# Scores and projections in split 16-bit halves, with weights scaled by bounds and a constant output scale, in a differential-attention block

## The reference, cut to what matters

```python
h = layernorm(x)
qkv = h @ Wqkv.T + b           # 16 query heads and 8 key heads of 128, 4 value heads of 256
p1 = softmax(causal(q1 @ k1.T / sqrt(128)))
p2 = softmax(causal(q2 @ k2.T / sqrt(128)))
o = (p1 - lam * p2) @ v        # 8 pairs of query heads, 256 wide
o = o * rsqrt(mean(o * o) + eps) * subln_w * (1 - LAMBDA_INIT)
x = x + layernorm(o @ out_w.T + out_b)
x = x + layernorm(ffn(layernorm(x)))
```

## Time and profile before

| | |
|---|---|
| median of 3 runs | 1268.17 us |
| the profiled execution, its own time | 1270.65 us |
| its span in the profile | 1268.8 us |
| mean granted clock of TensorE | 0.991 |
| PE busy | 1202.4 us (95%) |
| DVE busy | 1021.7 us (81%) |
| ACT busy | 997.8 us (79%) |
| POOL busy | 780.3 us (62%) |
| chain that ended last | PE 56%, DVE 17%, POOL 8%, issue 6%, ACT 5%, DMA 5% |

### The profile page before, as it was taken

How to read it: one execution, slowest core, us unless ns; L and a number is a source line. 1 busy time by engine, 2 the same in 40 slices (tenths; PEclk the granted TensorE clock), 3 DMA queues, 4 the chain that set the end, 5 groups by cost and what they waited for, 6 DMA issues and landing times.

```text
span 1268.8 us, 26516 instructions
## 1 busy us (share of the span) xinstructions
PE 1202.4 (95%) x8102; PEld 1011.7 (80%) x8102; DVE 1021.7 (81%) x2620; ACT 997.8 (79%) x2607; POOL 780.3 (62%) x1045
## 2 busy tenths in 40 slices
PE   7899999999999999999899999999998898999998
PEld 6788788888878888788788888788876787777887
DVE  6888988888779898988688888778788998846545
ACT  4799889988689989988688888887887898856341
POOL 3576666655657675646476575455567986776532
PEclk9999999999999999999999999999998998999999
DMA  3245554563266555534655554534563555540001
GB/s 130 65 78 103 88 97 93 93 103 71 45 122 105 88 95 90 107 58 64 121 86 91 88 96 85 101 55 82 117 105 86 90 99 94 97 88 1 29 18 38
DMA packets 368154, 106.62 MB, mean 84 GB/s; under 512 B 359312, under 2 KB 365712, under 8 KB 367504
## 3 DMA queue, kind: packets, MB, share of 16 engines
q1 hardware_dynamic: 366672, 103.37, 44.8%
q10 hardware_dynamic: 1344, 1.57, 0.4%
HBM read 14.71 MB, written 2.10 MB: 13 GB/s over the span
## 4 chain that ended last, share of the span: by engine, by line
PE 56%; DVE 17%; POOL 8%; issue 6%; ACT 5%; DMA 5%; SPq 1%; ACTq 0%; POOLq 0%; DVEq 0%
PE score_bank L1039 7%; PE score_bank L1173 6%; PE score_bank L1045 6%; PE score_bank L1042 6%; DVE p L1453 5%; DVE mx L1442 4%; POOL e_all L1736 3%; PE turn_bank L1066 3%; PE turn_bank L1067 3%; PE turn_bank L1068 3%; DMA oT<-o 3%; ACT e_all L1212 2%; DMA p16T<-p 2%; DVE score_bank L1437 2%; PE turn_bank L1119 2%
## 5 line engine op out<-in xcount | busy, mean ns | idle before, releaser
L1212 ACT ACTIVATE e_all<-score_bank,negmx 128x512 f32<-128x512 f32 (+2 forms) x640 | 393.6, 623 | 52.4 <-DVE negmx L1446 36.8
L1736 POOL TENSOR_TENSOR e_all<-e_all 128x512 f32<-128x512 f32 (+3 forms) x320 | 367.8, 1162 | 40.4 <-ACT e_all L1227 30.5
L1039 PE MATMUL score_bank<-k_hi,q_hi 128*128 128x512 f32 (+2 forms) x640 | 255.9, 400 | 27.8 <-ACT e_all L1212 15.5
L1453 DVE SCALAR_TENSOR_TENSOR p<-e_all,gain,p 128x512 f16<-128x512 f32 (+3 forms) x320 | 261.2, 831 | 11.3 <-ACT p L1234 10.5
L1442 DVE TENSOR_REDUCE mx<-score_bank 128x1 f32<-128x512 f32 (+1 forms) x384 | 242.1, 638 | 26.2 <-PE score_bank L1045 25.4
L1042 PE MATMUL score_bank<-k_lo,q_hi 128*128 128x512 f32 (+2 forms) x640 | 232.4, 363 | 0.4 <-DVE k_lo L1503 0.4
L1045 PE MATMUL score_bank<-k_hi,q_lo 128*128 128x512 f32 (+2 forms) x640 | 232.5, 363 | 0.0
L1234 ACT ACTIVATE p<-e_all,gain 128x512 f16<-128x512 f32 (+3 forms) x320 | 204.2, 666 | 20.4 <-POOL e_all L1736 19.7
L1781 POOL TENSOR_SCALAR ratio<-s,inv,neg_lam 128x1 f32<-128x1 f32 x128 | 55.9, 437 | 256.1 <-DVE inv L1724 255.8
L1039 PEld LDWEIGHTS score_bank<-k_hi,q_hi 128*128 128x128 f32 x640 | 121.3, 189 | 66.4 <-issue 27.5
L1066 PE MATMUL turn_bank<-v,p16T 128*128 128x256 f16 x567 | 157.1, 277 | 3.4 <-DVE o L1483 1.3
(11 more groups left out here) (391 smaller groups left out, 2789.0 us busy)
## 6 DMA issues: line engine op xcount, KB each, us to landing
p16T<-p SPq DMA_TRANSPOSE x320, 3.1
w_raw<-in_w_qkv_dram SPq DMA_DIRECT2D x3, 1024.0 KB, 5.4
w_raw<-in_w_o_dram SPq DMA_DIRECT2D x4, 512.0 KB, 3.3
oT<-o SPq DMA_TRANSPOSE x128, 2.5
bv<-in_hidden_dram SPq DMA_DIRECT2D x8, 256.0 KB, 3.0
w_raw<-in_w_ug_dram SPq DMA_DIRECT2D x4, 512.0 KB, 4.0
out_dram<-e SPq DMA_DIRECT2D x16, 128.0 KB, 1.7
e<-in_w_d_dram SPq DMA_DIRECT2D x1, 1024.0 KB, 6.2
```

The lines of the kernel that those rows point to most:

```text
L1039: pe.matmul(bank[:, 0:w], qh, kh, start=True, stop=False)
L1212: act.activation(e, S[k % NS][:, 0:w], ACT.Exp, bias=negmx[:, d % 2, m, s:s + 1], scale=-1.0 if alone else 1.0, accum_out=ssum[:, d % 4, s ...
L1453: dve.scalar_tensor_tensor(out=halves_of(q, w)[1], in0=e1_of(q, w), scalar=gain[:, d % 4, s:s + 1], in1=halves_of(q, w)[0], op0=ALU.mult, ...
L1736: pool.tensor_tensor(a, a, b, ALU.add).then_inc(p_pool, 1)
```

## The change

Input x (times a constant 8), the weights of q, k and v, and q and k themselves are stored as pairs of f16 halves in place of fp32r ones; the matmuls of scores and projections read these. Their number stays (CV has two small matmuls per group in place of one). The FFN's matmuls stay fp32r.

Since f16 has a small range, all three weights are scaled by bounds: per group there is a new step CQ (ACT, sum of squares of WQ), CV on DVE has five sums in place of two, CS on POOL takes the power of three numbers and scales the biases, and CU (DVE, four small instructions) gives `unit`, the factor by which a score must be multiplied. WQ, WK and WV now wait for CS. The exponential takes `unit` as a second pointer operand in 576 of 640 cases, and DVE multiplies the maximum by it (line 1466, 192 instructions that did not exist).

The outputs' halves OH and OL are scaled by the constant 2^-15; OH waits for the last PV alone. VE is gone from DVE; POOL adds the epsilon and multiplies (line 1758) ahead of its power (1761), and the result is applied at the sum into `acc` (1565). The FFN's input has storage of its own, so that its transposes wait for fewer late scores. The planner's costs change (exponential 0.23 to 0.32 us plus the same slope, scores and projections cheaper), and with them the order and the sharing of E2: 186 on ACT and 134 on POOL, where 205 and 115 were.

```diff
-SCORE_US, VALUE_US = 0.00136, 0.00257
+SCORE_US, VALUE_US = 0.00129, 0.00257
...
-                    add("E", "ACT", "E", (d, m, jj), 0.23 + 0.00084 * ww, [("DVE", "S", what)] + room, 1)
+                    add("E", "ACT", "E", (d, m, jj), 0.32 + 0.00084 * ww, [("DVE", "S", what)] + room, 1)
...
-                add("N", "DVE", "VE", o, 0.13, [("ACT", "SQ", o)], 0)
-                add("R", "ACT", "OH", o, 0.37, [("POOL", "OT", o)] + ([("SP", "OX", o - 4)] if o >= 4 else []), 0)
+                add("P", "ACT", "OH", o, 0.28, [pe] + ([("SP", "OX", o - 4)] if o >= 4 else []), 0)
...
-                    "WK": [("PE", "V", (g - 1, V_UNITS - 1))] if g else [], "WV": [("POOL", "CS", g)]}[kind]
+                    "WK": [("PE", "V", (g - 1, V_UNITS - 1))] if g else [], "WV": []}[kind] + [("POOL", "CS", g)]
...
-                        qh = q_hi[:, d // 2 % 2, s, m, at:at + P]
-                        kh = k_hi[:, m, key:key + w]
+                        qh = q16[:, d // 2 % 2, s, m, 0, at:at + P]
+                        kh = k16[:, d // DUOS % 2, m, 0, key:key + w]
...
                     act.activation(e, S[k % NS][:, 0:w], ACT.Exp, bias=negmx[:, d % 2, m, s:s + 1],
-                                   scale=-1.0 if alone else 1.0, accum_out=ssum[:, d % 4, s, m, c:c + 1]).then_inc(s_act, 1)
+                                   scale=-1.0 if alone else unit[:, g], accum_out=ssum[:, d % 4, s, m, c:c + 1]).then_inc(s_act, 1)
...
                     elif kind == "OH":
-                        act.wait_ge(rms_ready, o + 1)
+                        act.wait_ge(pv_done, last_part[o] + 1)
...
                         act.activation(o16[:, o % 4, 0:HID], bank_for("PV", o)[:, 0:HID], ACT.Copy,
-                                       scale=rms[:, o % 4:o % 4 + 1]).then_inc(o_hi, 1)
+                                       scale=O_SHRINK).then_inc(o_hi, 1)
...
-                            dve.tensor_reduce(negmx[:, d % 2, m, s:s + 1], mx[:, d % 2, m, s, 0:c + 1], X,
-                                              ALU.max, negate=True).then_inc(neg_ready, 1)
+                            dve.tensor_reduce(neg_raw[:, d % 2, m, s:s + 1], mx[:, d % 2, m, s, 0:c + 1], X,
+                                              ALU.max, negate=True).then_inc(raw_ready, 1)
+                            dve.wait_ge(raw_ready, neg_use[o, m] + 1)
+                            dve.tensor_tensor(negmx[:, d % 2, m, s:s + 1], neg_raw[:, d % 2, m, s:s + 1], unit[:, g],
+                                              ALU.mult).then_inc(neg_ready, 1)
...
                 def norm(o):
+                    pool.wait_ge(msq_ready, o + 1)
...
+                    pool.tensor_scalar(rms_b[:, c], msq[:, c], eps_v[:, g:g + 1], out_unit[:, g:g + 1], ALU.add, ALU.mult)\
+                        .then_inc(rms_step, 1)
                     pool.wait_ge(rms_step, o + 1)
                     pool.tensor_tensor(rms[:, c], rms_b[:, c], half_neg[:, 0:1], ALU.pow)\
                         .then_inc(rms_ready, 1)
```

More of the change, by code:

```diff
@@ L200, in spawn @@
             q = CHUNKS * d + j
-            add("S", "DVE", "S", what, (0.17 if last else 0.07) + 0.00104 * w + (0.15 if last and c else 0), [pe], 0)
+            unit = [] if d % DUOS else [("DVE", "CU", d // DUOS)]
+            add("S", "DVE", "S", what, (0.17 if last else 0.07) + 0.00104 * w + (0.25 if last and c else 0), [pe] + unit, 0)
             if last:
@@ L230, in spawn @@
         elif kind == "OP":
-            add("Q", "DVE", "OP", what, 0.4, [pe], 1)
+            add("Q", "DVE", "OP", what, 0.4, [pe, ("POOL", "OT", what)], 1)
             if what % (2 * DUOS) >= 2 * DUOS - 2 and what // (2 * DUOS) + 1 < GROUPS:
@@ L283, in spawn @@
         elif kind == "CQ":
-            add("Y", "DVE", "CV", what, 1.1, [], 1)
+            add("Y", "ACT", "CQ", what, 1.1, [], 1)
+            add("Y", "DVE", "CV", what, 2.4, [], 1)
         elif kind == "CS":
             add("Y", "DVE", kind, what, 0.2, [("PE", "CV", what)], 0)
-            add("Y", "POOL", kind, what, 1.6, [("DVE", kind, what)], 0)
+            add("Y", "POOL", kind, what, 2.8, [("DVE", kind, what)], 0)
+            add("Y", "DVE", "CU", what, 0.6, [("POOL", kind, what)], 0)
         elif kind == "N":
@@ L430, in needs @@
         if kind == "CV":
-            return [("DVE", "CV", what)]
+            return [("DVE", "CV", what), ("ACT", "CQ", what)]
         if kind == "OV":
@@ L434, in needs @@
         if kind == "F":
-            return [("DVE", "FH", what)] + ([("PE", "S", last_late_key)] if what < 2 else
-                                             [("PE", "QP", (ALL_DUOS // 2 - 1, 1, 1))] if what >= 4 else [])
+            return [("DVE", "FH", what)]
         if kind == "Z":
-            return [("ACT", "N", (what[0], 3, half)) for half in range(2)] + [("PE", "QP", (ALL_DUOS // 2 - 5, 1, 1))]
+            return [("ACT", "N", (what[0], 3, half)) for half in range(2)]
         if kind in ("G", "U"):
@@ L1050, in _ @@
                         bank = free_bank(kind, what)
-                        pe.matmul(bank[:, 0:1], ones[:, :], w_sq[:, what:what + 1], start=True, stop=True)\
-                          .then_inc(bound_full, 1)
+                        pe.matmul(bank[:, 0:3], ones[:, :], w_sq[:, :], start=True, stop=False)
+                        pe.matmul(bank[:, 0:3], ones[:, :], wb_sq[:, :], start=False, stop=True).then_inc(bound_full, 1)
                     elif kind == "PV":
@@ new lines, in _ @@
+                    elif kind in ("WQ", "WK", "WV"):
+                        n = ("WQ", "WK", "WV").index(kind)
+                        hi, lo = ((wq16[:, a, :, :], wkv16[:, a, :, 0:HID], wkv16[:, a, :, HID:2 * HID])[n]
+                                  for a in range(2))
+                        raw = w_raw[:, :, (0, BANK, BANK + HID)[n]:(BANK, BANK + HID, 2 * BANK)[n]]
+                        dve.wait_ge(w_hi, w_use[kind, what] + 1)
+                        dve.scalar_tensor_tensor(out=lo, in0=raw, scalar=w_scale[:, n:n + 1], in1=hi,
+                                                 op0=ALU.mult, op1=ALU.subtract).then_inc(w_lo, 1)
+                        if kind == "WQ" and what == 0:
+                            dve.tensor_scalar(subln_s[:, :], col[:, SUBLN_COL:SUBLN_COL + CT], 1.0 - LAMBDA_INIT,
+                                              None, ALU.mult).then_inc(subln_ready, 1)
@@ L1810, in _ @@
                     elif kind == "CS":
[L1811 to L1817 removed]
+                        g = what
```

359 lines of the change are left out of this document (186 added, 173 removed), and 8 rows, old and new, of the table FIRST_STEPS.

## The result

The change makes the kernel slower: 1292.94 us median against 1269.18 us for the kernel before on the same chip, a ratio of 1.0199 (95% interval 1.0169 to 1.0230). 1247 us had been forecast. The third rival of the prediction, the multiply as the bound, had 1285.

What follows compares the result with a forecast made beforehand. PE was taken as the bound: saving 36 us brings its steady work to 952 us, which at a 94% share gives 1013, 24 less than 1037. With +4.5 opening and -2 end, 1247 us was forecast, range 1228 to 1272.

Steps and rivals of the forecast that it cites:

- The third rival: Multiply of the maximum at line 1466, held by POOL, becomes the bound: PE's share 90.6%, 1285 us; chance 0.16.
- PE's gain: Scores and projections on PE in f16 save 36 us, taking its steady work from 988 to about 952 us.
- The proportional price: f16 matmuls on PE cost in proportion to columns: 0.2186 us at 512 columns, 0.164 at 384.
- The loads of ACT, DVE and POOL: Busy time in the steady stretch after the change: ACT about 913 us, DVE about 931, POOL about 736.
- the sum: Steady stretch: PE's 952 us at a 94% share give 1013 us; with +4.5 and -2 at the ends, 1247 us.
- the fuller stage: Stage from 1000 to 1117 us before the change: DVE and ACT at 87%, POOL 77%, PE only 90.6%.
- With four banks between them: In the score loop, exponential waits for the multiply, PE for the score bank it frees, with four banks between.
- The opening: First keys start near 20.2 us, since WK now waits for the bound and biases: +4.5 us, between 2 and 7.
- The output chain: OH waits for PV alone, so ACT's 22.1 us of waits should go; POOL's 0.651 us power is hidden.
- the 2 us taken off at the end: Between last PV and OH at the attention's end, SQ, VE and the power fall out: -2 us.
- The first rival: PE keeps its 95.3% share, as waits go and the plan with costs nearer the rows orders better: 1233 us; chance 0.17.

Runs made afterwards that it cites:

- the two forms that were meant to move the multiply: The change with earlier maxima scaled ahead of the last chunk's masking (1276.61 us), or scaled and handed to that masking as its start value (1286.86 us).
- the other opening: Biases' transfers ahead of the input's third block, weights' sums ahead of biases'; on the change with a pointer multiply 1264.45 us, against 1270.78 without.
- the three pairs: Kernels with biases' transfers and weights' sums first, against partners without: scaled in mask 2.7 us less, start value 6.5 less, pointer multiply 6.3 less.
- the constant scale: Change with queries' and keys' weights scaled by a constant, without their bounds, multiply or exponential's pointer: 1243.03 us with costs of before, 1246.15 us with the change's.

## Why the prediction was wrong, point by point

- **PE's gain**: right. The proportional price was nearly it (0.216 and 0.163 us measured, about 40 us by the distance between starts, where 36 were taken). The Trainium skill's figure ("TensorE: Matmul & The Clock Gate", back-to-back issue gap) was nearer still.
- **The loads of ACT, DVE and POOL**: right within 1%, the multiply's mean too (0.397 against 0.374 us). Not one of these sums is the cause.
- **The step that failed** is the sum's "Between the 95.3% of now and the 90.6% of the fuller stage I take 94%, nearer to the first". The share came out at 90.8%. The step turned all loads beside PE into one share, as if 72 us on DVE were worth what 53 us on ACT or 61 on POOL are. The runs give 39, 7 to 10 and 3 us for them, the last within the noise. DVE's sits between a tile's last maximum and the exponentials of all its chunks, which keep up to four score banks: from the last score to the bias it's 1.63 us without the multiply and 2.13 with it. ACT's is in the loop of the scores too, but with 0.09 us at each exponential; POOL's is not in it. That the place makes the difference, and not the engine, is argued from this: no run has the same work at two places of one engine, since the two forms that were meant to move the multiply left it in the way. "With four banks between them" did not cover it: 17 to 18 us are lost with a multiply that is never held.
- **The third rival** named the place, the mechanism and nearly the price. The held multiply's worth, 0.17 us each from which it decides, was passed in the mean: 39 us over 192 is 0.20 us. Its "Against", that the splits' mean excess is only 0.217 us, was no argument, since 0.217 us 192 times is 42 us. By the prediction's own 0.374 us for the multiply, twice the 0.17 from which it decides, it was worth more than the 0.16 that it got. That its share of 90.6%, taken over from another stage, lies so near the measured 90.8 is luck.
- **The opening**: 7.7 us where 4.5 were taken and 7 the end of the range. Missing were the output bias's transfer behind the same semaphore, and PE at half clock. The 3.5 to 4.5 us of it that the other opening takes back are worth 3 to 6 us in the end, by the three pairs.
- **The output chain**: right. ACT's 22 us for POOL's power are gone, and POOL's added instruction is hidden (3 us). Of the 2 us taken off at the end about one shows: from the start of the last score to the end of the span it's 164.2 us, 165.2 before.
- **The first rival**, that the plan orders better with the new costs, was wrong about the time. With the old costs the change is 44 us slower, but that costs nearer to the rows order better isn't shown by this: such costs made one kernel 6 us slower, and with the constant scale, where the costs of before are the nearer ones, 3 us faster. Nor is the new plan with the new instructions better than the old one with the old instructions.

Together: 49 for the multiply and the pointer (1292.94 less 1243.73), 3 to 6 for what the other opening takes back, against a change 24 us slower: 28 to 31 us of PE's 40 come out if these add up. The kernel that has none of the three, with the constant scale, gives 25. The difference, in a kernel at 93% PE, lies in waits that the runs don't separate.

## What to carry to other kernels

Cost an added instruction by the way it lengthens, not by its engine's load alone: one small link between the last input and what frees a buffer, at every tile, cost as much here (39 us) as the whole saving on the bounding engine, while 61 us of work on POOL, beside that way, cost 3. On an engine with a fixed order, an instruction put just ahead of a link can delay it as much as one behind it. Of two forms of a small vector instruction take the one that reads a single SBUF operand (a pointer on one column), and look at smallest, median and largest duration, not at the mean. When operands get a narrower type, try a constant scale that folds into weights before a bound that must be undone in the inner loop.
